# The residual of a feed-forward layer as one more product in PSUM, and one gate product for each pair of tiles

## The reference

```python
x = x + _L0_attn_a_ref(_layernorm(x, axis=-1), ...)
x = x + _L0_ffn_ref(_layernorm(x, axis=-1), w_gate, w_up, w_down)      # first feed-forward layer
x = x + _L0_attn_b_ref(_layernorm(x, axis=-1), ...)
x = x + _L0_ffn_ref(_layernorm(x, axis=-1), w_gate, w_up, w_down)      # second feed-forward layer

def _L0_ffn_ref(x, w_gate, w_up, w_down):          # H = 128, I = 352
    gate = fp4_linear(x, w_gate)
    y = fp4_linear(x, w_up)
    h = jax.nn.silu(gate) * y
    return fp4_linear(h, w_down)

def fp4_linear(x, w):                              # both rounded to a grid of FP4, in blocks of 16
    return jnp.einsum('bsk,nk->bsn', fp4_quant_dequant(x), fp4_quant_dequant(w))
```

## Time and profile before

| | us |
|---|---|
| median of 3 runs | 813.99 (813.62 to 816.39) |
| the profiled execution, whole | 816.01 |
| its span, first to last instruction | 814.3 |
| TensorE matmul busy | 615.5 (76%) |
| VectorE busy | 540.7 (66%) |
| ScalarE busy | 302.3 (37%) |
| GpSimd busy | 280.1 (34%) |

### The profile page before, as it was taken

The page is one execution under the profiler, slowest core; times in us unless marked ns, Lnnn a source line. Parts: engine busy times, 40 slices in busy tenths (PEclk is TensorE's granted clock), DMA queues, the critical chain, the costliest instruction groups (busy, mean ns, idle before and its releaser), DMA issues.

```text
span 814.3 us, 14007 instructions
## 1 busy us (share of the span) xinstructions
PE 615.5 (76%) x5231; PEld 445.5 (55%) x5231; DVE 540.7 (66%) x1126; ACT 302.3 (37%) x555; POOL 280.1 (34%) x328
## 2 busy tenths in 40 slices
PE   2376887888766667679777787798988988676886
PEld 1275875666633334378555565455655655454554
DVE  7615564333249948938889986666667666878784
ACT  2231111333224313412555545344444434455442
POOL 6540000000010000004558777534444445446454
PEclk9565998999989878969899998799999998899898
DMA  8400000000000000000000000000000000000000
GB/s 253 122 1 1 0 1 0 1 1 0 1 1 1 0 1 1 1 1 1 1 0 1 1 2 0 1 2 1 2 2 2 2 2 1 1 14 27 13 27 27
DMA packets 13676, 10.48 MB, mean 13 GB/s; under 512 B 1398, under 2 KB 12598, under 8 KB 13492
## 3 DMA queue, kind: packets, MB, share of 16 engines
q1 hardware_dynamic: 13620, 9.73, 4.2%
HBM read 7.63 MB, written 2.10 MB: 12 GB/s over the span
## 4 chain that ended last, share of the span: by engine, by line
PE 46%; DVE 21%; issue 14%; POOL 11%; ACT 7%; ACTq 0%; DMA 0%; POOLq 0%; DVEq 0%
PE ps L1157 6%; PE ps L1243 5%; PE ps L1374 4%; PE ps L1184 4%; PE ps L1272 3%; POOL G L276 3%; PE ps L1311 3%; DVE r L820 3%; PE ps L1393 2%; PE ps L1290 2%; PE ps L1193 2%; DVE S L828 2%; DVE arena L1017 2%; PE ps L1201 2%; POOL zT L279 1%
## 5 line engine op out<-in xcount | busy, mean ns | idle before, releaser
L1311 PE MATMUL ps<-wdT,xnt 128*128 128x128 f32 (+1 forms) x384 | 58.8, 310 | 45.5 <-ACT xnt L560 45.5
L1311 PEld LDWEIGHTS ps<-wdT,xnt 128*128 128x128 f32 (+1 forms) x384 | 52.5, 216 | 53.7 <-ACT xnt L560 53.3
L276 POOL TENSOR_TENSOR G<-S,hoff 128x704 f32<-128x704 f32 x32 | 48.6, 1518 | 80.5 <-DVE S L931 80.5
L1243 PE MATMUL ps<-G,xw 128*126 128x512 f32 x72 | 47.3, 810 | 30.1 <-ACT xw L505 22.4
L326 POOL TENSOR_TENSOR ln<-mv,lnc 128x4 f32<-128x4 f32 x64 | 13.0, 202 | 153.1 <-DVE mv L700 153.1
L345 POOL MEMSET early<- 128x2560 f32 x2 | 4.5, 2231 | 173.9 <-PE ps L1228 163.6
L553 ACT ACTIVATE xnt<-ps 128x352 f32<-128x352 f32 x64 | 29.7, 463 | 90.9 <-PE ps L1290 90.7
L365 POOL TENSOR_SCALAR_AFFINE_SELECT arena<-arena 128x1024 f32<-128x1024 f32 x32 | 34.9, 1092 | 71.5 <-ACT arena L637 71.5
L1017 DVE TENSOR_TENSOR arena<-ps,tri 128x1024 f32<-128x1024 f32 x32 | 39.2, 1225 | 23.4 <-PE ps L1374 23.4
L1290 PE MATMUL ps<-wguT,xnt 128*128 128x352 f32 x128 | 53.8, 503 | 1.0
L1292 PE MATMUL ps<-wguT,xnt 128*128 128x352 f32 x128 | 51.5, 485 | 3.9 <-DVE S L931 3.9
(11 more groups left out here) (199 smaller groups left out, 1525.0 us busy)
## 6 DMA issues: line engine op xcount, KB each, us to landing
X<-in_x SPq DMA_DIRECT2D x8, 256.0 KB, 4.9
out<-X SPq DMA_DIRECT2D x8, 256.0 KB, 2.3
wqkv<-in_wqkv SPq DMA_DIRECT2D x1, 1024.0 KB
band<-in_band SPq DMA_DIRECT2D x1, 897.8 KB
early<-in_wfc SPq DMA_DIRECT2D x1, 512.0 KB
kI<-in_scaled_eye SPq DMA_DIRECT2D x1, 192.0 KB
wattn<-in_wattn SPq DMA_DIRECT2D x1, 192.0 KB, 6.9
S<-in_wd SPq DMA_DIRECT2D x1, 176.0 KB, 3.6
```

Source lines behind the costliest of these rows:

```text
L276: tt(out=hgrid, in0=hmoved[k], in1=hoff[k][:, :], op=ALU.subtract).then_inc(s["fh_grid"], 1)
L1243: last = mm(ps[0:WI, w, :], xw[:, w * WO:w * WO + WI], G1[:, b, :], start=True, stop=True)
L1311: last = mm(ps[:, T_BANK + 1, k * P:(k + 1) * P], hT[r % 2][0:FK[c], k, c, :], wdT[0:FK[c], c, :], start=(c == 0), stop=(c == 2))
```

## The change

The down product of a tile gets a fourth product in its accumulation: the identity matrix times the tile of `X`, so that the sum in PSUM already holds the residual. In both layers ScalarE then copies the sum to `X`. The buffer `down`, GpSimd's addition in the first layer and VectorE's in the second fall away. VectorE multiplies silu and `up` once for each pair of tiles, which wants four buffers `sil` for two. The statistics of the first layer come one step earlier.

```diff
-        sil = [xnt[:, 20 * P + k * F:20 * P + (k + 1) * F] for k in range(2)]
+        sil = [xnt[:, 20 * P + k * F:20 * P + (k + 1) * F] for k in range(4)]
...
-        down_store = sb("down", [P, 4 * P])
-        down = [down_store[:, 2 * k * P:2 * (k + 1) * P].rearrange("p (k c) -> p k c", k=2) for k in range(2)]
...  GpSimd
-                def residual(r):
-                    g.wait_ge(s["f_down_copied"], ffn_pairs(p, r + 1))
-                    tt(out=X[:, 2 * r:2 * r + 2, :], in0=X[:, 2 * r:2 * r + 2, :], in1=down[r % 2],
-                       op=ALU.add).then_inc(s["f_x_done"], 1)
...
-                    if 0 <= r - 3 < PN:
-                        residual(r - 3)
...  ScalarE
                 def silu(t):
-                    need(a, "f_h", n - 1)
-                    act(sil[t % 2], ps[:, GATE_BANK, 0:F], ACT.Silu).then_inc(s["f_silu"], 1)
+                    need(a, "f_h", ffn_pairs(p, t // 2 - 1))
+                    act(sil[t % 4], ps[:, GATE_BANK, 0:F], ACT.Silu).then_inc(s["f_silu"], 1)
...
                 def down_copy(r):
                     a.wait_ge(s["f_down"], n + 1)
-                    need(a, "f_x_done", n - 1)
-                    act(down[r % 2], ps[:, T_BANK + 1, 0:2 * P].rearrange("p (k c) -> p k c", k=2), ACT.Copy).then_inc(s["f_down_copied"], 1)
+                    act(X[:, 2 * r:2 * r + 2, :], ps[:, T_BANK + 1, 0:2 * P].rearrange("p (k c) -> p k c", k=2), ACT.Copy).then_inc(s["f_x_done"], 1)
...
-                    if 0 <= r - 2 < PN and p == 0:
+                    if 0 <= r - 2 < PN:
                         down_copy(r - 2)
...  VectorE
-                def gated(t):
-                    n = ffn_tiles(p, t)
-                    v.wait_ge(s["f_silu"], n + 1)
-                    v.wait_ge(s["f_up"], n + 1)
-                    up = up_banks(t // 2)[:, t % 2, :]
-                    tt(out=up, in0=up, in1=sil[t % 2], op=ALU.mult).then_inc(s["f_h"], 1)
+                def gated(r):
+                    v.wait_ge(s["f_silu"], ffn_tiles(p, 2 * r + 2))
+                    v.wait_ge(s["f_up"], ffn_tiles(p, 2 * r + 2))
+                    k = 20 * P + 2 * F * (r % 2)
+                    tt(out=up_banks(r), in0=up_banks(r), in1=pair(xnt[:, k:k + 2 * F]), op=ALU.mult).then_inc(s["f_h"], 1)
...
-                def residual(r):
-                    v.wait_ge(s["f_down"], ffn_pairs(p, r + 1))
-                    tt(out=X[:, 2 * r:2 * r + 2, :], in0=ps[:, T_BANK + 1, 0:2 * P].rearrange("p (k c) -> p k c", k=2),
-                       in1=X[:, 2 * r:2 * r + 2, :], op=ALU.add).then_inc(s["f_x_done"], 1)
...
                     if 0 <= r < PN:
-                        gated(2 * r)
+                        gated(r)
                     if 0 <= r - 1 < PN:
                         move_h(r - 1)
                     if 0 <= r < PN:
-                        gated(2 * r + 1)
                         absmax_h(r)
...
-                    if p == 1 and 0 <= r - 2 < PN:
-                        residual(r - 2)
...
-                    if p == 0 and 0 <= r - 4 < PN:
-                        v.wait_ge(s["f_x_done"], ffn_pairs(p, r - 3))
-                        tile_stats(2, 2 * r - 8)
-                        tile_stats(2, 2 * r - 7)
+                    if p == 0 and 0 <= r - 3 < PN:
+                        v.wait_ge(s["f_x_done"], ffn_pairs(p, r - 2))
+                        tile_stats(2, 2 * r - 6)
+                        tile_stats(2, 2 * r - 5)
...  TensorE
                             last = mm(ps[:, T_BANK + 1, k * P:(k + 1) * P], hT[r % 2][0:FK[c], k, c, :], wdT[0:FK[c], c, :],
-                                      start=(c == 0), stop=(c == 2))
+                                      start=(c == 0), stop=False)
+                        last = mm(ps[:, T_BANK + 1, k * P:(k + 1) * P], eye[:, :], X[:, 2 * r + k, :], start=False, stop=True)
                     last.then_inc(s["f_down"], 1)
```

More of the change, by code:

```diff
@@ L905, in move_x @@
                     tt(out=xmoved, in0=ps[:, X_BANK, :], in1=xoff[:, :], op=ALU.add).then_inc(s["fx_moved"], 1)
-                def gated(t):
-                    n = ffn_tiles(p, t)
-                    v.wait_ge(s["f_silu"], n + 1)
-                    v.wait_ge(s["f_up"], n + 1)
-                    up = up_banks(t // 2)[:, t % 2, :]
-                    tt(out=up, in0=up, in1=sil[t % 2], op=ALU.mult).then_inc(s["f_h"], 1)
+                def gated(r):
[3 more added lines that the diff above has]
+                    tt(out=up_banks(r), in0=up_banks(r), in1=pair(xnt[:, k:k + 2 * F]), op=ALU.mult).then_inc(s["f_h"], 1)
                 def absmax_h(r):
-                    v.wait_ge(s["f_h"], ffn_tiles(p, 2 * r + 2))
+                    v.wait_ge(s["f_h"], ffn_pairs(p, r + 1))
                     reduce(out=pair(largest_h(r)), in_=blocks(up_banks(r)), axis=AX, op=ALU.max,
@@ L1047, in _ @@
             tile_stats(1, TILES - 1)
-            for r in range(PN + 4):
+            for r in range(PN + 3):
                 step0(r)
@@ L1300, in h_transposes @@
                         if k == 1:
-                            need(pe, "f_x_done" if p else "f_down_copied", n)
+                            need(pe, "f_x_done", n)
                         for c in range(3):
@@ L1431, in _ @@
             lin_transposes(1)
-            pe.wait_ge(s["f_down_copied"], PN)
+            pe.wait_ge(s["f_x_done"], PN)
             for n in range(TILES):
```

## The result

The changed kernel takes 829.53 us (median of 4 runs, 828.52 to 830.68), against 814.33 us before (4 runs): a ratio of 1.0183, 95% interval 1.0157 to 1.0208, slower by 15.2 us. A second measurement of the same kernel later gave 827.55 us and 1.0146 (1.0111 to 1.0180). The forecast was 823.6, with a range of 817 to 830, which the first median meets with half a us to spare; two of its four runs took 830.4 and 830.7.

The account below looks back on a forecast made before the run. The prediction took the round trip TensorE, ScalarE, TensorE through every down product as the bound, not VectorE. It added 7.1 us in the first layer and 2.5 in the second, 9.6 on 814.0: 823.6 us, range 817 to 830.

Parts of the forecast that it names:

- The ring TensorE, ScalarE, TensorE: Feed-forward layers: round trip from one down product to the next sets the step, 6.28 us even and 7.15 odd.
- The rival that followed the busiest engine: VectorE bounds the kernel, so relieving it makes the change faster: 24.8 us less, 789 us; chance 0.08.
- The price of two products, 0.53 for a pair: Two identity products added to each down product lengthen the step by 0.53 us at full clock, 0.98 at half.
- The 0.8 that I added to the second layer's first step: Second feed-forward layer: the first even step, 9.29 us before, grows by about 0.8, between 0.53 and 0.98.
- ScalarE's copy at nothing: The copy to X, new in the second layer, costs nothing where ScalarE waits for TensorE; at most 6.7 us uncovered.
- With VectorE out of the ring it should be 2.23 here too: Second layer: TensorE's idle time before odd steps' down products falls from 2.51 us to the first layer's 2.23.
- the spells go: Second layer: TensorE's half-clock stretches vanish from three slow even steps, which then take 6.81 us; case's chance 0.62.
- 3.1 us were booked as a gain in the second layer: Three slow even steps there get shorter by 0.98, 1.15 and 1.01 us, together 3.1 less.
- The joined gate product at nothing: VectorE's one gate product per pair saves 0.15 us, delays the clamp by up to 0.15; counted nothing mid-layer.
- I took 2.0 off: The profiled execution lay 2.0 us above the three runs' median, so 825.6 us became a median of 823.6.
- the forecast's own case: Whole kernel: added products lengthen the steps and half-clock stretches vanish; 823.6 us, 819 to 827, chance 0.62.
- the rival in which the spells stay in the second layer: Half-clock stretches remain in three even steps, each 8.6 us rather than 6.81: 5.4 us more, 829 us; chance 0.17.

Follow-up runs that it names:

- no_identity: The changed kernel without its 64 products with the identity, so both feed-forward layers leave the residual out of the sum: 812.36 us, 0.9972.
- gpsimd_residual: The changed kernel without products with the identity; in both layers ScalarE copies the down product to a buffer and GpSimd adds it to x: 811.98 us, 0.9940.
- gates_apart: The changed kernel with VectorE's gate products made one for each tile, as before the change: 823.12 us, 1.0081.
- changed_again: The changed kernel measured once more, unaltered: 827.55 us, 1.0146 of the kernel before.
- first_layer_only: The changed kernel, but its second feed-forward layer ends as before, with VectorE adding the residual; gate products joined in both layers: 824.96 us, 1.0112.
- gate_pair_only: The kernel before the change with only VectorE's gate products joined in pairs: 815.05 us, 1.0022.
- ratio_first: The kernel before with joined gate products and, in odd steps, VectorE's scale and ratio of h ahead of the clamp and sum of x: 818.41 us, 1.0021.
- gpsimd_ratio_first: The changed kernel without identity products, GpSimd adding the residual in both layers, and VectorE's ratio of h ahead of the clamp of x: 816.88 us, 1.0021.
- identity_twice: The changed kernel with each product with the identity made twice, so that twice x is added: 844.71 us, 1.0377.

## Why the prediction was right, and where its sizes were wrong

*What bounds it.* Right. The ring TensorE, ScalarE, TensorE sets the step; nothing that VectorE is spared shortens it much, and everything behind `hT_copy` lengthens it. The rival that followed the busiest engine would have gone for VectorE; no_identity, in which only VectorE's and GpSimd's relief is left, is faster by 0.3%, not by the 3% of that rival.

*The price of two products, 0.53 for a pair.* Too high: 0.44 to 0.45 (6.28 to 6.73, 7.15 to 7.60). I divided the 1.60 us of a row by six, but the next product starts before a row ends. In the kernel before, the gate product behind the down product of 448.28 has this row:

```profile
449.72 0.76 PE L1290 MATMUL ps<-wguT,xnt 128*128 128x352 f32 x2
```

From start to start the six take 1.44, 0.24 each, which would have made 0.48. In the changed kernel three products with `wdT` behind another product take 0.67 (725.76 to 726.43), 0.22 each like the ones with the identity. At half clock a product with the identity takes 0.42 (716.95 to 717.37), 0.85 for a pair instead of the 0.98 of the sum. The 0.8 that I added to the second layer's first step did not come, 9.27 (715.50 to 724.77) for 9.29, since half clock ended sooner: before, the transposes of `x` at 711.85, 5.1 us behind the down product, still take 1.06, and in the changed kernel those at 721.12, 5.6 behind, take 0.60.

*ScalarE's copy at nothing.* Right, by the rows at 727.45 to 729.29.

*"With VectorE out of the ring it should be 2.23 here too", and the spells go.* The idle time did become 2.23, and the inference fell. In the changed kernel the first layer, which had no spell past its first step, has two of 1.7 us each (8.38, and 8.40 from 463.26), and the second still has one of its three (8.40 from 746.70). The first step of the first layer grew by 1.2 for 0.5, from 7.77 to 9.00 (402.00 to 411.00). This is the step that failed: 3.1 us were booked as a gain in the second layer, of which a spell of 1.7 was left, and some 3.3 came as a loss in the first, for which the sum had nothing. The rows of the kernel before for its first layer are:

```profile
406.11 2.93 PE L1311 MATMUL ps<-wdT,xnt 128*128 128x128 f32 x12 [2.71 <-ACT xnt L560]
...
413.88 1.60 PE L1311 MATMUL ps<-wdT,xnt 128*128 128x128 f32 x12 [1.21 <-ACT xnt L560]
...
507.30 1.60 PE L1311 MATMUL ps<-wdT,xnt 128*128 128x128 f32 x12 [0.69 <-ACT xnt L560]
```

From the first down product to the last the first layer grew by 9.9 us (111.1 for the 101.2 from 406.11 to 507.30), and from its first down product to the end of the span the second grew by 3.7 (111.2 for 107.5). The forecast had 7.1 and 2.5.

The Trainium skill ("TensorE: Matmul & The Clock Gate", HAM oscillation) tells of a kernel whose waits for DMA, longer than the waits here, threw the clock back in every round of its loop. These traces show no such regularity: most odd steps behind 2.23 us of idle time run at full speed, and the trace of gpsimd_residual has none at half clock in odd steps whose idle time is longer.

*The joined gate product at nothing.* Right for the steps of the changed kernel: they are the same in gates_apart, because the ring with the two products on it is the longer chain. Without those products it loses 0.27 to 0.33 in odd steps, through the clamp of `x`. I had only the clamp of `h` in view, at "up to 0.15", and nothing for that of `x`.

*The sum.* 13.6 us by the two layers in the traces, 11.9 to 15.2 by the two measurements, 9.6 forecast. The price per pair was too high and the spells were counted as a gain, so two errors of opposite sign lie in it. Outside the layers the profiled executions differ by two terms that the sum had at nothing and that nearly cancel: the first down product comes 4.1 us earlier (402.00 for 406.11), and the linear attention takes 2.9 longer (202.4 for 199.5), which with 9.9 and 3.7 makes the 12.4 between the spans.

I took 2.0 off because the profiled execution before (816.0) lies above its median. No second trace of that kernel shows where these 2 us were, and the profiled execution of the changed kernel lies 1.0 below its median instead.

*The number.* 829.53 is outside the 819 to 827 that belonged to the forecast's own case, and beside the 829 of the rival in which the spells stay in the second layer (0.17). That rival did not come as it was told either: two of the three went there, and two new ones came in the first layer. The direction and the ring were foreseen; that the time falls within 817 to 830 owes something to luck.

*What stays open.* What decides a spell, and with it why two kernels with equal steps differ by 0.65%. The first layer's spells stand at the same steps in three traces that share this layer (from 432.94 and 463.26 in the changed kernel, and again in changed_again and first_layer_only), so they are not chance from run to run. With the gate products apart, the second of them comes one odd step later; I have no run that moves one on purpose. Nor is it shown why the linear attention is longer in the changed kernel: its two traces agree (202.4 and 202.3), but first_layer_only, which does the same work up to that place, takes 199.0.

## What to carry to other kernels

An engine that is busy 96% of a stretch need not set its pace. Follow one round of the pipeline from a product to the same product of the next step, and list which engines it passes; work saved beside it is worth little (0.3% here), and work added on it costs up to its full length in every step (1.7 to 2.1% for 64 products of 0.22 us, with what the clock adds). If a sum must go into PSUM by TensorE, put it ahead of the wait and not behind it: the same residual at the opening of the accumulation cost nothing that could be measured (0.9997 of before, 0.9971 to 1.0023). Take the price of a product from the start of one to the start of the next, not from the length of a row. And leave a margin in a forecast for the clock of TensorE: one stretch of unaltered code, 200 us long, differed by up to 4.7 between these kernels. Its mean granted clock was 0.91 to 0.92 in the five traces with 198.5 to 199.5 us and 0.88 to 0.90 in the five with 202.3 us and more.

## What the runs showed of the hardware

VectorE's clamp in place on bf16 numbers (128 x 512) took 0.26 us at its fastest and a median of 1.03 in gate_pair_only, where it stands beside GpSimd's subtraction. It ended 0.15 us behind the subtraction wherever it started beside it: 0.46 from 455.83 in the kernel before, 1.03 from 452.83 in gate_pair_only. In the second layer of ratio_first, where GpSimd does nothing beside it, it took 0.28 (721.65). VectorE's operations on f32 in PSUM beside the same subtraction kept their 0.89 us. The Trainium skill says that GpSimd's interfaces to SBUF are shared with VectorE, with contention for VectorE's instructions that run in a mode with two ports or have two inputs in SBUF ("GPSIMD Engine Reference", Specifications). These traces agree that there is contention, and show it as a wait for the end of GpSimd's instruction: 1.03 from 452.83, with GpSimd's 1.52 from 452.19. In which mode the clamp ran, no row shows.

A clock spell costs about 1.7 us in a step of 6.7 and came behind idle times of 2.23 as well as 2.51 us. Shorter steps had more of them in two pairs of traces (gate_pair_only and ratio_first, one and two; gpsimd_residual and gpsimd_ratio_first, none and four), but that is no rule: identity_twice, with longer steps than the changed kernel, has more of them too.
